# Gate and up blocks of a fused decoder block as seven-product 2x2 blocks over even and odd token tiles

## The reference

```
res = h
h2 = rmsnorm(h, ln2_w)
mlp = silu(h2 @ gate_w.T) * (h2 @ up_w.T) @ down_w.T
return res + mlp
```

## Time and profile before

| what | value |
|---|---|
| median of 3 runs | 427.8 us (427.33 to 429.48) |
| the profiled execution's own time | 427.6 us |
| its span, first to last instruction | 425.4 us |
| TensorE busy | 412.4 us, 97% |
| VectorE busy | 206.8 us, 49% |
| ScalarE busy | 162.9 us, 38% |
| GpSimd busy | 67.3 us, 16% |
| granted TensorE clock, mean | 0.995 of full speed |

### The profile page before, as it was taken

How to read it: one execution, slowest core, us unless ns; L and a number is a source line. 1 busy time by engine, 2 the same in 40 slices (tenths; PEclk the granted TensorE clock), 3 DMA queues, 4 the chain that set the end, 5 groups by cost and what they waited for, 6 DMA issues and landing times.

```text
span 425.4 us, 5205 instructions
## 1 busy us (share of the span) xinstructions
PE 412.4 (97%) x1908; PEld 326.8 (77%) x1912; DVE 206.8 (49%) x392; ACT 162.9 (38%) x334; POOL 67.3 (16%) x53
## 2 busy tenths in 40 slices
PE   7999999999989999999999999999999999999984
PEld 3878887666758888888888888888787888887763
DVE  3496971246674331313131313153455676676576
ACT  6768733935743522212222222343133133231231
POOL 3404303534562202020202020100000000000000
PEclk8999999999999999999999999999999999999999
DMA  7701111200020030303030312111100201201001
GB/s 251 245 2 50 51 49 51 67 32 2 1 99 2 35 114 19 130 6 131 12 121 27 103 45 99 49 49 51 49 21 30 74 26 49 75 25 50 26 0 74
DMA packets 10114, 25.41 MB, mean 60 GB/s; under 512 B 1681, under 2 KB 1809, under 8 KB 10098
## 3 DMA queue, kind: packets, MB, share of 16 engines
q1 hardware_dynamic: 8946, 23.10, 16.8%
q10 hardware_dynamic: 1152, 2.10, 1.3%
HBM read 23.10 MB, written 2.10 MB: 59 GB/s over the span
## 4 chain that ended last, share of the span: by engine, by line
PE 91%; DVE 5%; ACT 2%; issue 1%; ACTq 0%; DVEq 0%
PE bank L369 25%; PE bank L371 25%; PE bank L370 25%; PE bank L440 2%; PE bank L427 2%; PE bank L487 2%; PE bank L587 1%; PE bank L598 1%; PE bank L380 1%; PE bank L609 1%; PE bank L449 1%; PE bank L408 1%; DVE tmp L1190 1%; PE bank L470 1%; PE bank L569 1%
## 5 line engine op out<-in xcount | busy, mean ns | idle before, releaser
L369 PE MATMUL bank<-cols,ringS 128*128 128x512 f32 x304 | 119.5, 393 | 1.3 <-DVE cols L1027 1.3
L371 PE MATMUL bank<-cols,ringS 128*128 128x512 f32 x304 | 118.3, 389 | 0.0
L370 PE MATMUL bank<-cols,ringS 128*128 128x512 f32 x304 | 118.3, 389 | 0.0
L1157 DVE TENSOR_TENSOR big<-tmp,bank 128x512 f32 (+1 forms) x28 | 19.3, 688 | 103.0 <-ACT tmp L884 103.0
L369 PEld LDWEIGHTS bank<-cols,ringS 128*128 128x128 f32 x304 | 57.1, 188 | 14.3 <-issue 2.6
L370 PEld LDWEIGHTS bank<-cols,ringS 128*128 128x128 f32 x304 | 57.1, 188 | 12.1 <-issue 0.5
L371 PEld LDWEIGHTS bank<-cols,ringS 128*128 128x128 f32 x304 | 57.1, 188 | 11.9
L369 PE MATMUL bank<-wdS,cols 128*128 128x512 f32 x144 | 61.5, 427 | 0.0
L884 ACT ACTIVATE tmp<-bank 128x512 f32<-128x512 f32 x28 | 16.8, 598 | 105.6 <-PE bank L371 105.6
L371 PE MATMUL bank<-wdS,cols 128*128 128x512 f32 x144 | 56.4, 392 | 0.0
L370 PE MATMUL bank<-wdS,cols 128*128 128x512 f32 x144 | 56.2, 390 | 0.0
(11 more groups left out here) (147 smaller groups left out, 515.9 us busy)
## 6 DMA issues: line engine op xcount, KB each, us to landing
raw<-wstream SPq DMA_DIRECT2D x31, 512.0 KB, 3.3
rows<-x SPq DMA_DIRECT2D x8, 256.0 KB, 4.3
big<-ctxT SPq DMA_DIRECT2D x8, 256.0 KB, 2.6
big<-ctx SPq DMA_DIRECT2D x8, 256.0 KB, 3.0
out<-tmp ACTq DMA_DIRECT2D x8, 256.0 KB, 2.0
big<-ln_w SPq DMA_DIRECT2D x1, 256.0 KB, 5.3
big<-lora_b SPq DMA_DIRECT2D x3, 64.0 KB, 4.5
ga<-gate_lora SPq DMA_DIRECT2D x1, 72.0 KB, 5.1
```

Source lines behind the costliest of these rows:

```text
L369: pe.matmul(ps, a_hi, b_lo, start=first, stop=False)
L370: pe.matmul(ps, a_hi, b_hi, start=False, stop=False)
L371: return pe.matmul(ps, a_lo, b_hi, start=False, stop=last)
L1157: v.tensor_tensor(dst, blocks(hn[:, par, :]), blocks(bank[4 * par + 2 * hf + 1][:, :]), ALU.mult) \
```

## The change

Blocks m = 2 to 13 of gate and up are taken in 12 groups, g = 2 to 13: an even group is the gate of two m, the odd one after it the up of the same two m. A group is a 2x2 block product. The weights are four blocks, A11 and A12 (first m, first and second half of the 512 features), A21 and A22 (second m). The tokens are four blocks of 256 features by 512 tokens: B11 and B21 of the even tiles, B12 and B22 of the odd tiles. With four sums on either side,

The core of the diff:

```diff
+PRODUCTS = ((A11, B11), (S2, T2), (S1, T1), (S3, T3), (S4, B22), (A22, T4), (A12, B21))
+P1, P6, P5, P7, P3, P4, P2 = range(7)
+RING = (0, 1, 4, 5, 2, 3, 6, 7)
+SEQ = tuple((g, n) for g in range(G0, LAST_GATE) for n in range(7)) + (
+    (LAST_GATE, P1), (LAST_GATE, P6), (LAST_GATE, P5), (LAST_GATE, P7), (LAST_UP, P1), (LAST_GATE, P3),
+    (LAST_UP, P6), (LAST_GATE, P4), (LAST_UP, P5), (LAST_GATE, P2), (LAST_UP, P7), (LAST_UP, P3),
+    (LAST_UP, P4), (LAST_UP, P2))
...
 @block.gpsimd
+            for i in range(HB - 1):
+                t_low(i)
+            weight_sums(G0)
+            t_low(HB - 1)
+            for g in range(G0, N_GROUP):
+                if g + 1 < N_GROUP:
+                    weight_sums(g + 1)
+                else:
+                    for j in POOL_WD:
+                        wd_low(j)
+                if g % 2 == 1:
+                    up_product(g, 3, st_c22, c22[1])
+                    up_product(g, 1, st_c12, u4[1])
+                    if g < N_GROUP - 1:
+                        up_product(g, 2, st_c21, u2u3[1])
...
 @block.tensor
+            def strassen(g, n):
+                i, buf = g - G0, g % 2
+                a, m = PRODUCTS[n]
+                if n == 0:
+                    pe.wait_ge(g_lo, 4 * i + 2)
+                if n == 1:
+                    pe.wait_ge(g_lo, 4 * i + 4)
+                    if i == 0:
+                        pe.wait_ge(t_lo, HB)
+                free_bank(SEQ.index((g, n)))
+                for c in range(2):
+                    w = bass.ds(a * HALF_K + c * P, P)
+                    mm = three_pass(pe, product_bank(g, n), groupS[:, buf, 0, w], groupS[:, buf, 1, w],
+                                    setsS[:, m, 0, c, :], setsS[:, m, 1, c, :], c == 0, c == 1)
+                mm.then_inc(st_done, 1)
...
-            with pe.Fori(1, NM // 2) as j:
-                for hf in range(2):
-                    for par in range(2):
-                        if hf == 0:
-                            pe.wait_ge(ring_lo, 2 * j + (par - 1))
-                        pe.wait_ge(hid_ok, 4 * j + (2 * hf + par - 3))
-                        gate_up(par, hf)
+            for g, n in SEQ:
+                strassen(g, n)
...
 @block.scalar
+            hi_of_t(0)
+            hi_of_h2(B - 2)
+            f32_of_h2(B - 2)
+            hi_of_h2(B - 1)
+            f32_of_h2(B - 1)
+            hi_of_t(1)
+            hi_of_t(2)
...
 @block.vector
+            for g in range(G0, LAST_GATE):
+                weight_lo(g + 1)
+                make_u2(g)
+                make_u4(g)
+                sums_lo(g + 1, 0)
+                make_c22(g)
+                make_c12(g)
+                sums_lo(g + 1, 1)
+                make_c21(g)
+                make_c11(g)
+                if g % 2 == 1:
+                    up_first(g)
```

More of the change, by code:

```diff
@@ L69, in raw_slot, with group_load, wd_load, base_load @@
 def raw_slot(n):
-    return (n - LOOP_CHUNK) % RAW
+    return n % RAW if n < LOOP_CHUNK else (n - LOOP_CHUNK) % RAW
+def group_load(g):
+    return LOOP_CHUNK - G0 + g
+def wd_load(i):
+    return group_load(N_GROUP) + i
+def base_load(i):
+    return wd_load(NM // 2) + i
+def landed(n):
+    return 16 * sum(raw_slot(i) == raw_slot(n) for i in range(n + 1))
+def made(g, n):
+    return SEQ.index((g, n)) + 1
+def group_made(g):
+    return max(made(g, n) for n in range(7))
 def build(nc, x, ctx, ctxT, wstream, conv_w, conv_b, a_log, d_skip, dt_bias, ln1_w, ln2_w,
@@ L707, in hi_part @@
             def hi_part(n, dst):
-                landed = sum(raw_slot(i) == raw_slot(n) for i in range(n + 1))
-                act.wait_ge(raw_in[raw_slot(n)], 16 * landed)
+                act.wait_ge(raw_in[raw_slot(n)], landed(n))
                 act.activation(dst, raw[:, raw_slot(n), :], ACT.Copy).then_inc(w_hi, 1)
@@ L1139, in _ @@
                     gate_y(b)
[L1140 removed]
+                    low_y(b)
                 if b >= 3:
[L1142 removed]
+                    low_h2(b - 3)
                 if b >= 2:
@@ L1176, in _, with weight_lo @@
-            with v.Fori(0, NM // 2 - 1) as j:
-                pair(j)
-                ring_low(j, 1)
-            pair(NM // 2 - 1, last=True)
-            ring_low(NM // 2 - 1, 1)
+                v.tensor_tensor(hid_half(m, hf), by_parity(hn[:, par, :]), by_parity(bank[4 * par + 2 * hf + 1][:, :]),
+                                ALU.mult).then_inc(hid_ok, 1)
+            def weight_lo(g):
+                i, n, buf = g - G0, group_load(g), g % 2
+                for k, (lo, hi) in enumerate(((0, D), (D, D + HALF_K))):
+                    src = raw[:, raw_slot(n), 0:D] if k == 0 else raw[:, raw_slot(n), D + HALF_K:2 * D]
+                    v.wait_ge(g_hi, 3 * i + k + 1)
+                    v.tensor_tensor(groupS[:, buf, 1, lo:hi], src, groupS[:, buf, 0, lo:hi].bitcast(F32), ALU.subtract) \
+                        .then_inc(g_lo, 1)
@@ new lines, in sums_lo, with combine @@
+            def sums_lo(g, k):
+                i, buf = g - G0, g % 2
+                q = bass.ds(D + HALF_K + k * D, D)
+                v.wait_ge(g_hi, 3 * (i + 1))
+                if i == 0 and k == 1:
+                    v.wait_ge(gu_done, 3)
+                v.tensor_tensor(groupS[:, buf, 1, q], sums[:, bass.ts(k, D)], groupS[:, buf, 0, q].bitcast(F32),
+                                ALU.subtract).then_inc(g_lo, 1)
+            def combine(g, n, dst, other, done, op=ALU.add):
+                v.wait_ge(st_done, made(g, n))
+                v.tensor_tensor(dst, other, product_bank(g, n), op).then_inc(done, 1)
@@ new lines, in _ @@
+            for g in range(G0, LAST_GATE):
+                weight_lo(g + 1)
[9 more added lines that the diff above has]
+                    up_first(g)
+            weight_lo(LAST_UP)
+            make_u2(LAST_GATE)
+            make_u4(LAST_GATE)
+            sums_lo(LAST_UP, 0)
```

519 lines of the change are left out of this document (402 added, 117 removed).

## The result

The changed kernel takes **422.1 us** (median of 4 runs, 421.48 to 423.51) against 428.6 us for the kernel before on the same chip: ratio 0.9852, 95% interval 0.9826 to 0.9878. It is faster, by 1.5%, and the whole interval lies under 1. The prediction had the sign right and the size wrong: 415.3 us was forecast, half of the expected gain is missing, and 422.1 lies outside the range of 411 to 421. The profiled execution took 421.5 us.

The account below looks back on a forecast made before the run. TensorE, busy 97% of the span, was taken as the bound, each matmul removed worth 0.227 us. Terms -16.3 + 0.8 + 0 + 1.0 + 0.5 + 1.5 = -12.5 gave 415.3 us against the median, range 411 to 421.

Parts of the forecast that it names:

- The loop: Gate/up loop: 576 matmuls become 504 at 0.227 us each, with no stall; -16.3 us.
- 7.5 named as the sign: Sign for the loop: VectorE busy about 7.5 us a group.
- Last transposes: Token sums at b = 8 ahead of tile 7's scaling delay the last transposes; +1.0 us, bounds 0 and +2.5.
- Scan loop: Weight low parts moved to b = 1 and 2, old TensorE wait shrinks; 0 us, bounds -1 and +2.
- First four calls: First gate/up calls: 96 matmuls of 512 columns become 192 of 256 at 0.118 us; +0.8 us, bounds 0 and +2.
- The mark of 0.13: Sign of being wrong: 256-column matmuls standing over 0.13 us apart.
- First group: Second product of the first group waits for token-sum and weight-sum low parts; +0.5 us, bounds 0 and +3.
- Handoff: Loop to down: tile 0 on time, tile 1's split +1.1, some slip; together +1.5 us, bounds 0 and +4.
- B: Rival: handoffs cost much more, two of the last four terms at their upper ends; 418 to 424 us, chance 0.18.
- C: Rival: VectorE becomes the bound through collisions with GpSimd, 10.9 us a group, slower than before; 432 us, chance 0.04.
- A: Rival: no handoff costs, all terms after the first two are 0; 412.3 us, range 411 to 412.5, chance 0.15.
- Rival D: Gain absent: each of 84 products pays 0.2 us for waits and its bank, 16.8 in all; 428 us, chance 0.03.

Follow-up runs that it names:

- e9: e8 with VectorE's token sums of b = 8 left ahead of the last scaling, as in e2; 412.7 us.
- e3: Changed kernel with GpSimd's list in the loop reordered: weight sums behind the first of an up group's three multiplications, not the third; 419.9 us.
- e4: Changed kernel with GpSimd's gate x up multiplications replaced by memsets to zero, leaving out three quarters of those products; 419.3 us.
- e2: Changed kernel with GpSimd's first token-sum low part waiting until VectorE's last scaling is done; 419.4 us.
- e1: Changed kernel with the first gate and up weights' high and low parts back at b = 3 and 4, as before the change; 427.7 us.
- e5: Changed kernel with the first gate and up weights' high and low parts both at b = 0, behind tile 2's decays; 421.3 us.
- e8: Changed kernel with e3, e5 and e6 together, and ScalarE's tail table load moved ahead of tile 0's last high part; 417.6 us.
- e6: e2 with VectorE's token sums of b = 8 moved behind the last scaling; 422.9 us.

## Why the prediction was wrong

Step by step, with the term that was forecast. One of the prediction's own signs of being wrong came true: TensorE waits for VectorE in the middle groups.

- **The loop, -16.3, "with no stall": the step that failed.** The price was right: 0.227 each within and between products, shown by e9. The stalls were 3.7 us. The forecast added up each engine's work for a group (VectorE 6.9 us and 1.0 of collisions of 9.52) and took the rest as cover. What it never did was follow one group's weights through all the lists. That chain crosses GpSimd, ScalarE and VectorE, and on GpSimd an up group's sums were queued behind three multiplications that wait for the results of the up group before (e3, e4). The low part was said to be needed "some 7 us after it can be made"; that was read from VectorE's list alone. Collisions were mis-sized as well: 0.22 us was allowed for each. They cost 0.37 (e4), and VectorE is busy for 108.8 of the 126 us from 158 to 284, 8.2 of each 9.5 us where 7.9 was summed and 7.5 named as the sign. They lengthen the chain; without GpSimd's order they would have stayed within the cover, which e3 shows.
- **Last transposes, +1.0: 2.8.** The four sums and the scaling behind them were foreseen, and e2's 0.7 us is what they cost. Overlooked was GpSimd's first token-sum low part, which the forecast has as "done before" 143.6 without a place; it began at 140.27, because ScalarE's high part of pair 0 stands in its list ahead of the high parts of tiles 6 and 7 and waits for nothing there. The forecast had named this mechanism for other places and not looked for it here.
- **Scan loop, 0 within -1 to +2: +1.1.** The collision at b = 1 was foreseen with 0.4 us reaching TensorE. It was 0.8 us of wait and, in this execution, 1.6 us at the lower clock behind it, of which 0.8 was left at the first gate and up call; without the lower clock that call comes 0.3 us later than before (e2), the old wait of 1.3 being gone. Putting the operation back is far worse (e1), a free stretch of GpSimd is better (e5).
- **First four calls, +0.8: +1.4.** From 143.69 to 158.17 stand 120 matmuls of 256 columns, 0.1207 us each, not 0.118. 192 x 0.1207 - 21.8 = 1.4. The mark of 0.13 was not passed. The section of the Trainium skill that the prediction sets beside its rows (TensorE: Matmul & The Clock Gate, Back-to-back issue gap) gives N/2.4 + 2.5 ns there as the gap of a single matmul, not of a stream with weight loads; this case's 227 and 120.7 ns lie above it by 11 and 12.
- **First group, +0.5: 0.** TensorE passes the second product of group 2, where the wait was to be, at its usual distance.
- **Handoff, +1.5: +0.9.** Down of tile 0 was on time. Tile 1's split made TensorE wait 0.84 us, with 1.1 forecast, for the reason given: ScalarE reached it behind the last chunk and its table load (e8). The 0.7 us lost in the rest of the tail is not assigned to a cause; it is there in e3, e8 and e9 as well (133.0 to 133.1 us from tile 1's down to the end, 132.4 before), 0.2 of it in the matmuls and 0.5 behind VectorE's last instruction.

Sum of the misses against the span: 3.5 us ahead of the loop, 3.2 in it, 0.6 less at the handoff, 0.7 more in the tail, 6.8 in all; the span fell by 5.7 where 12.5 was forecast.

Of the rivals, B (handoffs at their upper ends, 418 to 424) has the right time and half of the mechanism, given 0.18. C's collisions cost more than forecast and less than it takes for VectorE to become the bound. A, no handoff costs at all, 412.3 us: e9 reaches 412.7, in part by terms that cancel (1.1 us won in the scan loop; 0.6 lost in the first calls, 0.7 at the last transposes and 0.7 in the tail). Rival D's arithmetic does not fit: 0.2 us for each of 84 products on top of 415.3 would be 432, not 428.

## What to carry to other kernels

Room on each engine is not cover. For each thing that the bound engine will wait for, follow its chain through every list it crosses and write down what stands ahead of it in each, with that thing's own releaser; work that waits for the results of one group must not stand ahead of work that the next group needs first. And where VectorE operations with two SBUF inputs stand beside long GpSimd ones that read SBUF, check the start of each against the other one by one: here 0.1 us of difference in their start decided over 2 us (e2), and moving one instruction handed the collision to its neighbour (e6).
